# Router products and filler products move into the matmul engine's waits before the feed-forward part; one chunk and three weight pieces change place in the queues behind it

## The reference

```
logits = x_flat @ W_router
probs = jax.nn.sigmoid(logits)
topk_probs, topk_idx = jax.lax.top_k(probs, TOPK)
...
out = sq_relu(x_flat @ W_sh_up) @ W_sh_down
for e in range(E):
    h = sq_relu(x_flat @ W_up[e])
    out = out + combine[:, e:e + 1] * (h @ W_down[e])
```

## Time and profile before

| | before |
|---|---|
| median of 3 runs | 126.13 us (124.91 to 127.34) |
| the profiled execution's own time | 124.76 us |
| its span | 123.0 us |
| PE busy | 113.9 us, 93% of the span, 1171 matmuls |
| ACT, DVE, POOL busy | 75.8, 89.6, 59.1 us |
| mean granted TensorE clock | 0.984 |
| chain that ended last | PE 85%, DVE 6%, POOL 4%, issue 2%, ACT 1% |

### The profile page before, as it was taken

How to read it: one execution, slowest core, us unless ns; L and a number is a source line. 1 busy time by engine, 2 the same in 40 slices (tenths; PEclk the granted TensorE clock), 3 DMA queues, 4 the chain that set the end, 5 groups by cost and what they waited for, 6 DMA issues and landing times.

```text
span 123.0 us, 3129 instructions
## 1 busy us (share of the span) xinstructions
PE 113.9 (93%) x1171; PEld 91.1 (74%) x1171; DVE 89.6 (73%) x241; ACT 75.8 (62%) x167; POOL 59.1 (48%) x65
## 2 busy tenths in 40 slices
PE   3989999999999999999996969999999999999980
PEld 2357757686869676776674859989998999999980
DVE  0679898227969686967664469999579999999442
ACT  4013527983677566871941766999768988986300
POOL 6397242351965289251011041637957794673110
PEclk9999999999999999999999996799999999999999
DMA  3899999769969995992000000032892000000002
GB/s 117 236 316 374 406 426 392 248 247 290 351 185 424 344 419 142 418 347 80 0 5 0 0 3 0 5 53 87 241 303 101 3 0 0 5 0 0 0 0 85
DMA packets 6198, 20.46 MB, mean 166 GB/s; under 512 B 776, under 2 KB 2344, under 8 KB 6184
## 3 DMA queue, kind: packets, MB, share of 16 engines
q1 hardware_dynamic: 6040, 20.14, 46.3%
q10 hardware_dynamic: 144, 0.13, 0.3%
HBM read 19.99 MB, written 0.28 MB: 165 GB/s over the span
## 4 chain that ended last, share of the span: by engine, by line
PE 85%; DVE 6%; POOL 4%; issue 2%; ACT 1%; DVEq 0%; POOLq 0%
PE RA L378 6%; PE K L304 5%; PE C L293 5%; PE K L440 3%; PE C L556 3%; PE C L646 3%; PE C L553 3%; PE RA L331 3%; PE C L552 3%; PE K L556 3%; PE K L552 3%; PE K L553 3%; PE RA L552 3%; PE M L402 3%; PE RA L556 3%; PE RB L388 2%
## 5 line engine op out<-in xcount | busy, mean ns | idle before, releaser
L881 POOL TENSOR_TENSOR hl<-craw,hh 128x448 fp32r<-128x448 f32 (+2 forms) x12 | 12.9, 1073 | 12.8 <-ACT hh L799 12.8
L845 POOL TENSOR_TENSOR rstd<-vpe,mhalf 128x1 f32<-128x1 f32 (+1 forms) x10 | 5.8, 583 | 23.5 <-DVE vpe L980 23.5
L881 POOL TENSOR_TENSOR wul<-wraw,wuh 128x768 fp32r<-128x768 f32 x6 | 10.9, 1822 | 8.4 <-ACT wuh L693 8.4
L881 POOL TENSOR_TENSOR wdl<-wraw,wdh 128x768 fp32r<-128x768 f32 (+1 forms) x6 | 9.9, 1653 | 3.3 <-ACT wdh L693 3.3
L926 POOL TENSOR_TENSOR kT<-kT,qT 128x448 f32<-128x448 f32 x7 | 8.1, 1152 | 5.8 <-DVE qT L1261 5.8
L785 ACT ACTIVATE rt<-RA 128x448 f32<-128x448 f32 (+2 forms) x17 | 8.5, 498 | 1.2 <-PE RA L556 0.9
L799 ACT ACTIVATE hh<-craw 128x448 fp32r<-128x448 f32 (+2 forms) x16 | 7.9, 503 | 1.3 <-DVE craw L1222 1.2
L785 ACT ACTIVATE rt<-RB 128x448 f32<-128x448 f32 (+2 forms) x15 | 7.7, 517 | 0.7 <-PE RB L556 0.7
L378 PEld LDWEIGHTS RA<-kT,qT 64*64 64x64 f32 x256 | 7.1, 134 | 0.8 <-issue 0.8
L378 PE MATMUL RA<-kT,qT 64*64 64x56 f32 x256 | 7.6, 221 | 0.0
L965 DVE STREAM_TRANSPOSE rft<-rf 128x384 f32<-128x384 f32 x8 | 4.6, 575 | 3.5 <-ACT rf L684 3.4
(11 more groups left out here) (185 smaller groups left out, 338.1 us busy)
## 6 DMA issues: line engine op xcount, KB each, us to landing
craw<-ctx_nat SPq DMA_DIRECT2D x8, 780.0 KB, 6.2
craw<-ctx_tr SPq DMA_DIRECT2D x8, 768.0 KB, 5.7
wraw<-w_up SPq DMA_DIRECT2D x6, 384.0 KB, 6.2
wraw<-w_down SPq DMA_DIRECT2D x5, 384.0 KB, 3.4
craw<-share SPq DMA_DIRECT2D x7, 224.0 KB, 4.3
pk<-pack SPq DMA_DIRECT2D x1, 388.0 KB, 4.9
pk<-pack SPq DMA_DIRECT2D x1, 256.0 KB, 2.8
wde<-w_down SPq DMA_DIRECT2D x1, 256.0 KB, 6.5
```

The lines of the kernel that those rows point to most:

```text
L845: pool.tensor_tensor(dst, src, mhalf[:, 0:src.shape[1]], ALU.pow).then_inc(S[done], 1)
L881: pool.tensor_tensor(dst, src, high.bitcast(F32), ALU.subtract).then_inc(S[done], 1)
```

## The change: what it does

```diff
-LATE_AT = (8, 13, 21)
-LOW_AT = (5, 8, 13, 21)
+LATE_AT = (8, 14, 21)
+LOW_AT = (8, 11, 14, 21)
-WARM_Y3 = 2
+WARM_Y3, WARM_GATE = 5, 2
...
         def on_pool(c):
-            return c % 8 in (1, 3, 7) and c < NSP - 1
+            return c % 8 in (1, 5, 7) and c < NSP - 1
...
-                for _ in range((0, 2, 0, 2, 1, 2, 1, 3)[b]):
+                for _ in range((0, 2, 0, 2, 1, 2, 1, 2)[b]):
...
                 sp.dma_start(cb[:, e, :], share[e:e + 1, :, :].rearrange("e b t -> e (b t)").broadcast_to([128, NT])).then_inc(s_cb[e > 1], 16)
             weights(k)
+            weights(k + 1)
...
-            for c in range(3):
+            for c in range(4):
                 up_high(c, 0, done)
+            pe.wait_ge(S["x1"], PAIRS)
+            for q in range(p):
+                router(q)
             y2_transpose(p)
-            up_high(3, 0, done)
+            pe.wait_ge(S["kvs"], B)
+            keep_warm(1)
             query_features(p)
...
-            pe.wait_ge(S["kvs"], B)
             cross_out(p)
             up_low(2, 0, done).then_inc(S["up"], 1)
             up_low(3, 0, done)
-            for q in range(p):
-                router(q)
             down_high(0)
             keep_warm(WARM_Y3)
             y3_transpose(p)
+            keep_warm(WARM_GATE)
...
-                if c == 3:
+                if c == 4:
                     pe.wait_ge(S["cmb"], 1)
```

More of the change, by code:

```diff
@@ L264, in _ @@
                 context_n(b)
-                for _ in range((0, 2, 0, 2, 1, 2, 1, 3)[b]):
+                for _ in range((0, 2, 0, 2, 1, 2, 1, 2)[b]):
                     weights(k)
                     k += 1
-            assert k == 2 * NPC - 1
+            assert k == 2 * NPC - 2
             sp.wait_ge(S["cT"], 1)
```

## The result

| | before | changed |
|---|---|---|
| median | 125.64 us (124.91 to 127.34, 4 runs) | 127.72 us (127.34 to 128.81, 4 runs) |
| profiled execution | 124.76 us | 127.34 us |
| its span | 123.0 us | 125.2 us |
| mean granted clock | 0.984 | 1.000 |

The changed kernel is slower: the ratio is 1.0235, with a 95% interval of 1.019 to 1.0281, so a loss is certain and one of over 2% is not. Executions of a kernel that took over 1.5% more than its fastest are left out of the ratios in this document; in the table that is the kernel before's 127.34 us, without which the two medians would be 125.16 and 127.72 us. The forecast was 127.2 us.

What follows compares the result with a forecast made beforehand. PE, without holes from 73 to 119 us, was taken to set the end, so its waits count in full. Piece 10's 2.4 us, with PE's gains already included, added to the profiled 124.76 us gave 127.2 us, range 124.9 to 129.2.

Steps and rivals of the forecast that it cites:

- Routers and fillers at no cost: PE around the transposes of y2 and y3: added instructions fit into existing holes, cost 0 to 0.2 us, taken as 0.
- The clock stays up, 1.71 us saved on PE: PE after 74.71 us: filled holes prevent the 3.42 us stretch at 1.2 GHz, saving 1.71 us.
- Choosing steps 1.8 us earlier, at 79.3: DVE's sums: without POOL's chunk 3 subtraction and piece 8 beside them, they end some 1.8 us earlier, about 79.3 us.
- Chunks 11, 19, 27 to DVE and 13, 21, 29 to POOL, cost 0: Subtractions swapped between DVE and POOL: both keep their counts and DVE catches up, costed at 0.
- `share` and broadcasts 0.8 us earlier: ACT's copy 0.3 us earlier plus 0.5 us without piece 10 ahead: broadcasts issued from 84.1 us, at DVE by 88.2.
- without that piece `share` takes 1.7 us: Issue of `share` to first broadcast: 1.7 us instead of 2.21 without piece 10 in front, 0.5 us gained.
- Piece 10 lands at 94.2 and costs 2.4 us: Load issued behind seven broadcasts at 87.3 us makes ACT, then POOL, wait; PE's last product of chunk 15 2.4 us late.
- POOL's order as second in line, 0.3 us: POOL's expert 1, pieces 9 and 10 among subtractions: lead used up at chunk 13, 0.3 us lost at chunk 15.
- What lies around the span: Time outside the span: no term given to it; the sum was made on the profiled execution's 124.76 us.
- The rivals: Alternatives to the forecast (0.44): clock lost too 0.22, piece in time 0.18, faster 0.11, nothing happens 0.05.
- a lower clock behind the stop: PE's stop around 94 to 96 us also brings a low clock, 1.0 to 1.7 us more, about 128.5 us; chance 0.22.
- case 3: Transfers behind the broadcasts speed up by 3 us, piece 10 lands in time, POOL's order costs 0.3: 125.1 us; chance 0.18.

Runs made afterwards that it cites:

- e1: Kernel before with only PE's border edits (routers ahead of the transpose of y2, fillers 1, 5 and 2); ratio 1.0011 to the kernel before.
- e10: e1 with the turn of the weights on PE one chunk later; ratio 1.0065 to the kernel before, median 126.06 us.
- e9: e8 with chunks 3, 11, 19, 27 back on POOL and 5, 13, 21, 29 on DVE; ratio 1.0055 to the kernel before, median 125.88 us.
- e8: e7 with DVE's step for the first routed expert one chunk later; ratio 0.9934 to the kernel before, median 124.36 us.
- e7: Changed kernel, POOL's piece 8 at chunk 3, piece 9 at 8, piece 10 loaded ahead of `share`, its steps at 17; ratio 0.9991, median 125.24 us.
- e5: Kernel before with only piece 10's load moved behind the broadcasts; ratio 1.0515 to the kernel before, profiled execution 133.49 us.
- e2: Changed kernel with piece 10's load issued after two broadcasts instead of seven; ratio 1.011 to the kernel before, profiled execution 125.98 us.
- e3: Changed kernel with ACT's and POOL's steps for piece 10 three chunks later, load still late; ratio 1.0049 to the kernel before, profiled execution 126.11 us.
- e4: Changed kernel without its eight fillers; ratio 1.0476 to the kernel before, 130.16 to 132.88 us.
- e6: e2 with POOL's pieces 8 and 9 back at chunks 5 and 8; ratio 1.0058 to the kernel before, profiled execution 125.90 us.

## Why the prediction was right, step by step

- **Routers and fillers at no cost:** right. Start of the last transpose 71.58 against 71.62 us.
- **The clock stays up, 1.71 us saved on PE:** right for PE, 1.6 us at chunk 3. In the kernel before it was no gain to be had: e1 and e10 show DVE's choosing steps behind it, which take 1.05 to 1.16 us of PE. The prediction did not price this, and did not need to, since the same change takes POOL's steps away from them; e9 against e8 shows what that is worth.
- **Choosing steps 1.8 us earlier, at 79.3:** right, they end at 79.16 (81.30 before).
- **Chunks 11, 19, 27 to DVE and 13, 21, 29 to POOL, cost 0:** wrong, without effect on the sum. DVE's subtraction of chunk 11 now stands behind its wait for the broadcasts, and PE's lead falls from 1.0 to 0.3 us there; e8, which takes it out of that wait, has 0.86 us at chunk 11 where e7 has 0.48. POOL's subtractions of chunks 7 and 9, the latter behind piece 8, had by then taken 0.6 us of the lead, which the prediction does not have either. It has the whole lead used up by POOL at chunk 13. The sum was spared because the load's landing, and not the lead, dates PE behind chunk 13.
- **`share` and broadcasts 0.8 us earlier:** half of it wrong. ACT's copy started at 81.66 us (81.76 forecast), but `share` took the same 2.21 us to the first broadcast as before. Piece 10's load in front of it had not delayed it, so the step "without that piece `share` takes 1.7 us" was 0.5 us off. DVE had the broadcasts at 88.73 us, not 88.2.
- **Piece 10 lands at 94.2 and costs 2.4 us:** right in kind and size. It was issued at 87.71 us (87.3 forecast) and used at 93.94, 6.2 us later where the forecast had 6.9; the two errors nearly cancel, which is luck. PE started chunk 14's last product at 96.45 us (96.6 forecast) and chunk 15's at 97.85 (98.1). e5 shows the mechanism alone, e2 takes 1.4 us back by the load's place, e3 takes PE's later holes away by the step's place.
- **POOL's order as second in line, 0.3 us:** right in kind. e2, with the load in time, has PE's last product of chunk 15 at 96.46 us, 0.75 us behind the kernel before and not 0.3; POOL added the expert at 89.44 us and not at 88.9, which is the half us of the broadcasts.
- **What lies around the span:** missed. I took 1.8 us as given. It is 2.14 to 2.21 us in the changed kernel's runs, so 0.4 us of the 2.6 us between the profiled executions lie outside of the span. The span alone grew by 2.2 us where 2.4 were forecast. That the profiled execution came out 0.1 us from the forecast is in part luck: 0.2 too much inside of the span against 0.4 outside of it that the forecast lacks. The median of the runs, 127.72 us, is 0.5 us above it.
- **The rivals:** a lower clock behind the stop did not occur in the profiled execution, but it exists (e5); one of the four executions, 128.81 us, had a clock of 0.987, and no trace shows where it fell. Transfers fast enough to have the piece in time would have made case 3; the piece took 6.2 us, near the 6.3 and 6.5 us of the earlier trace rows.

## What to carry to other kernels

Before a hole in the bounding engine is filled, follow what the next engine will do with the time: here a lead of 1.6 us was used up by POOL's queue and by a wait on DVE before a transfer turned it into a loss, and only when all three were moved (e7, e8) did a gain of 0.7% remain. A load that moves behind others is to be priced at the step that waits for it, with all that is queued behind that step on its engine; moving the step (e3) can be as good as moving the load (e2). Small vector steps between SBUF tiles want a stretch in which POOL is idle.

## What the runs showed of the hardware

- Time outside of the span goes with the program: 1.75 to 1.87 us in every run of the kernels with chunks 1, 3 and 7 of eight on POOL (before, e1, e5, e9, e10), 2.11 to 2.21 in those with 1, 5 and 7 (changed, e2, e3, e4, e6, e7, e8). e9 differs from e8 in that one line. Why is open.
- Without fillers the granted clock fell for twice as long as before (e4), although PE was busy without a hole from 74 us on. The kernel before also had executions with a clock of 1.00 throughout, so the fall at this border is not the same in every execution.
- From the issue of the 14 KB write to HBM to the issue of the first broadcast, which waits for its landing, 2.21 us passed with 384 KB in flight ahead of it in the queue (before: 82.68 to 84.89) and without (changed: 82.28 to 84.49).
- A DVE step on SBUF tiles that takes 0.19 us beside an idle POOL took 1.71 us beside a POOL step of 1.89 us, and ended 0.05 us behind it (e9 against e8).
